# A transformer layer on one core: where the rotary products of the queries stand, and which engine takes the last query tile

## The reference

```python
q = (hidden_states @ wq).reshape(B, S, H, D)
k = (hidden_states @ wk).reshape(B, S, Hkv, D)
v = (hidden_states @ wv).reshape(B, S, Hkv, D)
q = q * cos + _rotate_half(q) * sin
k = k * cos + _rotate_half(k) * sin
scores = jnp.einsum('bqkgd,bskd->bkgqs', qg, k) * scale
attn = jax.nn.softmax(scores, axis=-1)
out = jnp.einsum('bkgqs,bskd->bqkgd', attn, v).reshape(B, S, E)
x = _layernorm(x + out @ wo)
x = _layernorm(x + _L0_ffn_ref(x, ...))
```

## Time and profile before

| what | us |
|---|---|
| median of 3 runs | 897.87 |
| lowest and highest run | 894.81, 898.11 |
| the profiled execution, its own time | 896.11 |
| span of the profiled execution | 894.3 |
| busy in the span: TensorE (matmul) | 876.0 |
| VectorE | 743.9 |
| ScalarE | 711.1 |
| GpSimd | 268.9 |

### The profile page before, as it was taken

The page is one execution under the profiler, slowest core; times in us unless marked ns, Lnnn a source line. Parts: engine busy times, 40 slices in busy tenths (PEclk is TensorE's granted clock), DMA queues, the critical chain, the costliest instruction groups (busy, mean ns, idle before and its releaser), DMA issues.

```text
span 894.3 us, 16211 instructions
## 1 busy us (share of the span) xinstructions
PE 876.0 (98%) x5658; PEld 457.9 (51%) x5658; DVE 743.9 (83%) x1655; ACT 711.1 (80%) x929; POOL 268.9 (30%) x232
## 2 busy tenths in 40 slices
PE   9999999999999999999999999999999999999996
PEld 3334444444444444434444444444436888888885
DVE  5688999999999999999999999999955455665545
ACT  2466999999999999999999999999985466555564
POOL 6564430045334010001001000210104665665555
PEclk9997999999999999999999999999999999999998
DMA  8874543423342122122223212121112010110001
GB/s 301 251 208 103 148 116 89 98 73 86 103 115 58 46 77 71 52 70 67 53 60 82 74 43 78 45 69 31 35 55 57 25 49 24 48 48 25 25 24 48
DMA packets 53458, 69.98 MB, mean 78 GB/s; under 512 B 17344, under 2 KB 26560, under 8 KB 53376
## 3 DMA queue, kind: packets, MB, share of 16 engines
q1 hardware_dynamic: 50280, 65.53, 26.4%
q0 software_dynamic: 864, 3.15, 1.1%
q10 hardware_dynamic: 2232, 0.25, 0.2%
HBM read 46.74 MB, written 16.25 MB: 70 GB/s over the span
## 4 chain that ended last, share of the span: by engine, by line
PE 89%; DVE 5%; ACT 2%; SPq 2%; DMA 2%; issue 1%; POOL 0%; POOLq 0%; DVEq 0%
PE pv_bank L1395 27%; PE ring_bank L1305 24%; PE pair_bank L1454 13%; PE pair_bank L1524 12%; PE pv_bank L1550 3%; PE ring_bank L1550 3%; PE ring_bank L1405 2%; DVE block_max L869 2%; PE pair_bank L1343 1%; ACT probs L1203 1%; DMA ident<-identity 1%; PE ring_bank L1420 1%; DMA k_max<-k_parts 0%; PE pair_bank L1305 0%; DVE inv_sums L962 0%
## 5 line engine op out<-in xcount | busy, mean ns | idle before, releaser
L1203 ACT ACTIVATE probs<-pair_bank 128x1024 f32<-128x1024 f32 x512 | 495.9, 1024 | 45.6 <-PE pair_bank L1454 45.5
L869 DVE TENSOR_REDUCE block_max<-ring_bank 128x1 f32<-128x384 f32 x854 | 486.5, 609 | 14.4 <-PE ring_bank L1305 4.1
L1305 PE MATMUL ring_bank<-k_max,q_sb 48*128 48x512 f32 x1122 | 310.1, 443 | 3.8 <-DVE block_max L865 2.6
L1305 PEld LDWEIGHTS ring_bank<-k_max,q_sb 48*128 48x128 f32 x1122 | 149.1, 185 | 267.1 <-DVE block_max L869 119.7
L1395 PE MATMUL pv_bank<-probs,v_all 128*17 128x512 f32 x2048 | 271.4, 602 | 0.7 <-ACT probs L1203 0.7
L1454 PE MATMUL pair_bank<-q_sb,k_sb 50*128 50x512 f32 x1024 | 221.5, 427 | 0.8 <-ACT probs L1203 0.7
L1063 DVE SCALAR_TENSOR_TENSOR hid<-pair_bank,up_s,silu 128x512 f32<-128x512 f32 x63 | 47.1, 748 | 85.1 <-ACT silu L1265 85.1
L1454 PEld LDWEIGHTS pair_bank<-q_sb,k_sb 50*128 50x128 f32 x1024 | 98.5, 186 | 27.2 <-ACT probs L1203 6.4
L774 POOL TENSOR_TENSOR hid_l<-hid,hid_h 128x512 fp32r<-128x512 f32 x63 | 81.7, 1296 | 86.4 <-ACT hid_h L1244 85.7
L689 POOL TENSOR_TENSOR attn<-attn,inv_rows 128x1024 f32<-128x1024 f32 x7 | 16.7, 2388 | 300.8 <-DMA inv_rows<-inv_d 300.8
L865 DVE CUSTOM_DVE_ANT_0 above<-ring_bank,above 128x512 f32<-128x512 f32 x128 | 88.1, 689 | 5.0 <-ACT above L1151 4.9
(11 more groups left out here) (147 smaller groups left out, 862.9 us busy)
## 6 DMA issues: line engine op xcount, KB each, us to landing
k_max<-k_parts SPq DMA_DIRECT2D x96, 96.0 KB, 3.1
q_sb<-q_parts SPq DMA_DIRECT2D x64, 128.0 KB, 2.8
k_sb<-k_parts SPq DMA_DIRECT2D x96, 64.0 KB, 2.4
attn<-xT SPq DMA_DIRECT2D x8, 512.0 KB, 7.6
q_parts<-high SPq DMA_DIRECT2D x16, 256.0 KB, 3.6
q_parts<-low SPq DMA_DIRECT2D x16, 256.0 KB, 3.9
q_sb<-q_parts SPq DMA_DIRECT2D x64, 64.0 KB, 2.9
attn<-pv_sb SPq DMA_DIRECT2D x128, 32.0 KB
```

Source lines behind the costliest of these rows:

```text
L869: dve.reduce_max(block_max[half % 2][:, col:col + 1], bank[:, 0:width], axis=AX.X).then_inc(ring_used, 1)
L1203: act.activation(probs[t % 2][:, 2 * pr:2 * pr + 2, :], pair_bank[pr][:], ACT.Exp, scale=D ** -0.5).then_inc(probs_ready, 1)
L1305: pe.matmul(bank[:, 0:last - first], q_sb[k][rows, i, qt * P:(qt + 1) * P], k_max[k // QH][rows, kind * CH + first:kind * CH + last], star ...
```

## The change

It has four pieces.

1. In every step of the prologue VectorE does the products of a query half ahead of the maxima of the same place, not after them. ScalarE copies V and K rows of tiles 3, 5 and 7 before high_part of the tile before (it was after it).
2. The second half of the last query tile isn't multiplied by VectorE. ScalarE copies pv_bank to q_last in SBUF (copy_q_last, after hook 3 of tile 7). GpSimd makes the two products (products_last), rotates, rounds (high_last) and subtracts. The first P x V waits for the copy.
3. The four early banks are taken in another order, so that the last two differences that ScalarE takes lie in pair_bank[1]; the second scores of step 0 wait for these two. In step 0 TensorE issues them ahead of max block 1.
4. On GpSimd products_k(1) moves behind turn 1. On SyncE the wait for all query stores and swap_strips(1) move behind load_shift(0, 1); the stores of tile 7 go out high parts first.

```diff
         q_bank = [pair_bank[0][:, 0, :], pair_bank[0][:, 1, :]]
-        early_banks = [ring_bank[0][:], ring_bank[1][:], pair_bank[1][:, 1, :], pair_bank[1][:, 0, :]]
+        early_banks = [ring_bank[1][:], pair_bank[1][:, 1, :], pair_bank[1][:, 0, :], ring_bank[0][:]]
         k_bank, v_bank = ring_bank[2], pv_bank
...
         def bank_index(pos):
-            return pos % EARLY_BANKS if pos < early_entries else (0, 1, EARLY_BANKS)[pos % BANKS]
+            return pos % EARLY_BANKS if pos < early_entries else (3, 0, EARLY_BANKS)[pos % BANKS]
...
                 cols = slice(c * CH, (c + 1) * CH)
-                for part, buf, ready, count in [((0, high, hi_ready, 2 * m + j + 1), (1, low, lo_ready[j], m + 1))[q] for q in parts]:
+                highs = (0, high, last_high_ready, j + 1) if m == BLOCKS - 1 else (0, high, hi_ready, 2 * m + j + 1)
+                for part, buf, ready, count in [(highs, (1, low, lo_ready[j], m + 1))[q] for q in parts]:
                     sp.wait_ge(ready, count)
...
                             load_kv(0, 1)
-                            swap_strips(1)
-                        store_q(m, 0)
-                        store_q(m, 1)
+                            for part in range(2):
+                                store_q(m, 0, (part,))
+                                store_q(m, 1, (part,))
+                        else:
+                            store_q(m, 0)
+                            store_q(m, 1)
                     if m == 2:
...
-            for slot in range(4):
-                sp.wait_ge(stored[slot], 16 * 2 * B)
-            sp.wait_ge(v_used, 2 * B)
+            def prologue_over():
+                for slot in range(4):
+                    sp.wait_ge(stored[slot], 16 * 2 * B)
+                sp.wait_ge(v_used, 2 * B)
...
                         load_shift(p + 1, 0)
+                    if first and k == 0:
+                        prologue_over()
+                        swap_strips(1)
                     if first and k < B - 1:
...
+            def products_last():
+
+                cols = slice(CH, S)
+                pool.wait_ge(q_last_ready, 1)
+                pool.wait_ge(q_tables_loaded[1], 16 * 2)
+                pool.wait_ge(rot_ready, 2 * (BLOCKS - 1))
+                pool.tensor_tensor(by_sin[0][:], q_last, sinq_sb[:, cols], ALU.mult).then_inc(q_last_parts, 1)
+                pool.tensor_tensor(by_cos[1][:], q_last, cos_sb[:, cols], ALU.mult).then_inc(q_last_parts, 1)
+
             def rotate(m, j):
-                pool.wait_ge(parts_ready, Q_PARTS * m + 3 + j)
+                if m == BLOCKS - 1:
+                    pool.wait_ge(parts_ready, Q_PARTS * m + 2)
+                    pool.wait_ge(q_last_parts, j + 1)
+                else:
+                    pool.wait_ge(parts_ready, Q_PARTS * m + 3 + j)
                 if m:
...
                     after_turn(0)
-                pool.wait_ge(hi_ready, 2 * m + j + 1)
+                if m == BLOCKS - 1:
+                    pool.wait_ge(last_high_ready, j + 1)
+                else:
+                    pool.wait_ge(hi_ready, 2 * m + j + 1)
                 pool.tensor_tensor(low[slot][:], rotated[j][:], high[slot][:].bitcast(fp32), ALU.subtract).then_inc(lo_ready[j], 1)
...
+            def high_last(j):
+                slot = 2 + j
+                pool.wait_ge(rot_ready, 2 * (BLOCKS - 1) + j + 1)
+                pool.wait_ge(stored[slot], 16 * 2 * (B - 1))
+                pool.tensor_copy(high[slot][:], rotated[j][:]).then_inc(last_high_ready, 1)
+
             for m in range(BLOCKS):
+                if m == BLOCKS - 1:
+                    products_last()
                 rotate(m, 0)
                 rotate(m, 1)
+                if m == BLOCKS - 1:
+                    high_last(0)
+                    high_last(1)
                 if m == 0 or m % 2 or m >= FIRST:
...
                     rotate_k(0)
-                if m == BLOCKS - 2:
-                    products_k(1)
+            after_turn(1)
+            products_k(1)
             for b in range(1, B):
...
                     low_first(m - 1)
+                rotary_q(m, 0)
                 early_maxima(m, 2)
-                rotary_q(m, 0)
                 early_maxima(m, 3)
-                early_maxima(m, 4)
                 if m < BLOCKS - 1:
                     rotary_q(m, 1)
+                early_maxima(m, 4)
                 early_maxima(m, 5)
...
                         turn_shift(before)
-                    if n == 3 and g == 0:
-                        rotary_q(BLOCKS - 1, 1)
                     if key:
...
+            def copy_q_last():
+                act.wait_ge(proj_ready, 3 * BLOCKS)
+                act.activation(q_last, pv_bank[:], ACT.Copy).then_inc(q_last_ready, 1)
+
             def take_v(b):
...
                     gap_high()
+                if c and b:
+                    copy_v_rows(b)
+                    copy_k_rows(b)
                 if m:
...
                 early_takes(m, 1)
-                if c:
-                    if b:
-                        copy_k_rows(b)
-                    copy_v_rows(b)
+                if m == 1:
+                    copy_v_rows(0)
                 early_takes(m, 2)
...
                     early_takes(m, h)
+                    if (m, h) == (BLOCKS - 1, 3):
+                        copy_q_last()
...
                                 difference(*maxima_at(g))
-                            if (g, pr) == (2, 1):
-                                high_part(BLOCKS - 1, 0)
-                            if (g, pr) == (3, 1):
-                                high_part(BLOCKS - 1, 1)
                             if n + 1 < HALVES * PAIRS:
...
                 if g == 0:
-                    pe.wait_ge(parts_ready, Q_PARTS * BLOCKS)
+                    pe.wait_ge(q_last_ready, 1)
                 if t == 0 and not first_use:
...
                                 if pr:
-                                    for index in range(2, EARLY_BANKS):
+                                    for index in (1, 2):
                                         pe.wait_ge(*taken(last_in(index, early_entries)))
...
                             maxima(0)
-                            maxima(1)
                             scores(1)
-                            for i in range(2, len(entries)):
+                            for i in range(1, len(entries)):
                                 maxima(i)
...
                             maxima(0)
```

More of the change, by code:

```diff
@@ L108, in layer @@
         by_sin = [sb(f"by_sin{c}", [P, CH], fp32, one) for c in range(2)]
+        rotated = [sb(f"rotated{c}", [P, CH], fp32, one) for c in range(2)]
+        q_last = attn[:, FIRST, 0:CH]
+        key_signs = sb("key_signs", [P, HKV * D], fp32, one)
+        high = [sb("high0", [P, CH], f32r, one)]
         v_rows = [sb(f"v_rows{c}", [P, CH], fp32, one) for c in range(2)]
-        rotated = [sb(f"rotated{c}", [P, CH], fp32, one) for c in range(2)]
-        key_signs = sb("key_signs", [P, HKV * D], fp32, one)
-        high = [sb(f"high{c}", [P, CH], f32r, one) for c in range(4)]
+        high += [sb(f"high{c}", [P, CH], f32r, one) for c in range(1, 4)]
         low = [sb(f"low{c}", [P, CH], f32r, one) for c in range(4)]
@@ L194, in layer @@
         k_gap_ready = sem("k_gap_ready")
+        q_last_ready, q_last_parts, last_high_ready = sem("q_last_ready"), sem("q_last_parts"), sem("last_high_ready")
         k_stored = [sem(f"k_stored{b}") for b in range(B)]
```

## The result

| | before | changed |
|---|---|---|
| median of 20 runs each, us | 896.56 | 899.28 |
| lowest and highest | 894.57, 899.18 | 895.75, 902.0 |
| profiled execution: own time, span | 896.11, 894.3 | 895.75, 893.9 |
| mean granted clock of the profiled execution | 0.991 | 0.995 |

The ratio of the changed kernel to the kernel before is 1.0031 (95% interval 1.0023 to 1.0040): **slower by 0.3%, some 2.8 us**. The prediction was 897.7 for a kernel at 897.87, no change, with 0.2 us won. The measured change is a loss, and its interval does not reach 1.

The account below looks back on a forecast made before the run. The prediction took the kernel to be bound by TensorE's stream; 6.1 us won up to turn 1 less 4.6 for SyncE's queue gave 1.5, taken as 0.2 for the clock: about 897.7, no measurable change (0.55), range 895 to 900.

Parts of the forecast that it names:

- Part 1: Prologue, query products ahead of maxima and earlier V and K copies: counted zero, bounds 0.7 lost and 0.5 won.
- Part 2: Banks and last query tile at steps 0 and 1: step 1's scores at 68.0, 1.75 us earlier.
- Part 4: SyncE's queue after turn 1: a new 2.8 us stall at step 16; the way to step 24 is 4.6 longer.
- T: The end of turn 1 on VectorE, from which the queue is counted; forecast 79.0, before 85.12.
- Part 3: Clock at steps 0 and 1: no fall, at 4 in 5, winning 4.4 us besides the 1.75.
- the lost half-clock stretch: Steps 1 to 5 took 13.83 us where the later pace gives 9.44; the episode cost 4.4.
- The term: Lead up to turn 1: 4.4 from the clock together with 1.75 from step 1, 6.1 us earlier.
- The sum: 6.1 won less 4.6 for the queue: 1.5 us won if the clock holds in the stalls, 0.2 taken.
- my middle: Clock after the stall at step 16, bounds 0 and 4.4: between 1.5 won and 1.1 lost, 0.2 won taken.
- Rival B: Clock still falls before step 5, only 1.75 won, queue takes 4.6: 2.9 lost, median 900.8; chance 0.20.
- Rival A: SyncE's queue is in time, no stall at steps 16 and 24: all 6.1 remain, median 891.8; chance 0.18.
- Rival C: Clock holds at step 16 and falls at step 24: 2.9 lost, 900.8; chance 0.07.

Follow-up runs that it names:

- The fourth experiment: The changed kernel with products_k(1), swap_strips(1) and the order of the prologue put back as before; 893.51 us, ratio 0.9964 to the kernel before.
- The first experiment: The changed kernel with products_k(1) and swap_strips(1) put back where they were; 893.51 us, ratio 0.9965 to the kernel before.
- The ninth experiment: The first experiment plus one extra matmul of 256 columns ahead of the second scores in step 0; 892.65 us, ratio 0.9966 to the kernel before.
- the fifth experiment: The changed kernel plus two unread matmuls ahead of the wait for the shift in steps 16 and 24; 897.49 us, ratio 1.0013 to the kernel before.
- The second experiment: The kernel before with only products_k(1) moved behind turn 1 and swap_strips(1) behind the shift of half 1; 902.64 us, ratio 1.0069.
- the seventh experiment: The changed kernel with SyncE's shifts of halves 2 and 3 ahead of swap_strips(2) and swap_strips(3); 900.75 us, ratio 1.0042 to the kernel before.
- sixth: The first experiment plus extra matmuls in step 0, 256 columns ahead of the second scores and 128 behind each later max block; 892.37 us, ratio 0.9953.

## Why the prediction was wrong

**Part 1 (prologue: zero) held.** The fourth experiment puts it at nothing that can be told. The first scores came at 64.15, forecast 64.4, and the loss in tile 5 that the bounds allowed for is there: TensorE was held up near 46, and part of it was won back.

**Part 2 (banks, last tile) held.** Second scores at 65.41 (forecast 65.4), step 1 at 68.17 (68.0). GpSimd was done at 72.9 (bound 74), and nobody waited for it.

**Part 4 (the queue) held to 0.6 us**, as the numbers behind T show, and the first two experiments confirm that it is the cause of the loss: with the keys early the stalls are gone, with the keys late alone they come to the kernel before. What I gave as 4.6 from turn 1 to step 24 measured 128.56 - 80.43 - 43.46 = 4.67.

**Part 3, the clock at the hand-over, is the step that failed.** I wrote: "So I expect no fall, at 4 in 5", because TensorE would idle about 1.0 us of the 3.6 from 64.4 on. The idle time came nearly as forecast (2.47 us busy in 64.4 to 68.0, so 1.1 idle), and the clock fell all the same, to 0.55 in 69 to 72. So it was not the chain to step 1 that was wrong but what I concluded from it. With the fall, the 4.4 that I put on the lost half-clock stretch was not to be had in full. In the best trace the stretch was shorter, and step 5 came 83.58 - 79.14 = 4.4 earlier, of which 1.6 were already there at step 1 and 2.9 are clock. Over many executions it is less. The first experiment shows the lead alone, with no stall behind it: 3.1. The term stood at 6.1, twice as much. The ninth experiment shows that the size was fair for a clock that holds, 5.6 at step 5 in its trace, and that the clock is what was missing: its executions with the higher mean clock are 2.8 faster than the others. The two rows that I had for it (42% idle with a fall, 45% without one) contradict each other already, and I still took 28% as safe. They were slices of 3 us besides, and the 1.16 us for which TensorE idled before 66.32 in the kernel before lay mostly in the slice ahead of the one I read. What decides between a fall and none stays open.

**The sum.** The measured lead and the queue make 3.1 - 4.7 = 1.6 lost; the fifth experiment, which has the queue's delay and little of the clock behind it, has 1.2 lost (0.0013 of 896). The clock behind the stalls adds 1.6, between the bounds of 0 and 4.4; my middle amounted to 1.3. The last two add up to the measured 2.8 because they are differences of the same ratios; with the 1.6 from the lead and the queue it is 3.2, so 0.4 is left over. A second way agrees: the queue's 4.6 and the clock's 1.6 make 6.2, and that is what the two moves cost the kernel before (6.2) and nearly what they cost the changed one (5.9). So the queue and the clock behind it were sized rightly, and the error of 3.0 (0.2 won, 2.8 lost) is the lead, 3.1 in place of 6.1.

The time itself, 899.28, lies inside my range of 895 to 900. That is luck: the range stood around a kernel at 897.87, which 20 runs put at 896.56, and the loss is real. I had also said that a measurement can tell only 4.5 us from no change; with 20 runs of each the interval is 2.1 to 3.6 us.

Rival B named the mechanism: the clock still falls before step 5, the queue takes its 4.6. Its 2.9 lost is almost the measured 2.8, but partly by luck: it had 1.75 for the lead (3.1 measured) and nothing for the clock behind the stalls (1.6), and the two errors nearly cancel. A middle case, a fall that ends sooner, was in neither the forecast nor the rival. Rival A (the queue in time) is ruled out by the trace. Rival C (a fall at step 24 and none at step 16) can't be told apart from falls at step 16, since the changed kernel's trace has neither.

The Trainium skill, TensorE: Matmul & The Clock Gate, section HAM oscillation — how this bites in real kernels, tells of waits for a DMA after which TensorE ran at the lower clock. The second experiment's trace agrees (0.62 busy in 111 to 114, clock 0.54 in 114 to 117); the changed kernel's own trace has two such waits and the clock stays at 1.00 (1.10 busy in 105 to 108, 0.84 in 126 to 129). Both happen with the same kind of stall.

## What to carry to other kernels

Before a transfer is moved behind another one in a queue, lay the queue out from the event that starts it to the next deadline of the busiest engine. Here that sum, from issue and landing times, was right to 0.6 us, and it says that swap_strips(1) should stay in the time that SyncE had to spare: the change without that move and that of products_k(1) beats both kernels (0.9965). Count a wait for a round trip (DMA, addition, DMA) inside the queue as a piece of its own: it held SyncE for 2.87 us in the changed kernel and 3.85 in the seventh experiment, where the issue of four DMAs takes 2.3 to 2.7. And don't book a clock stretch as won because a hole gets smaller: keep both ends, since it was worth half its price here, and look at the mean clock of many executions, not at one trace.

## What the runs showed of the hardware

The clock fell at the hand-over with TensorE recorded as busy 2.40 of 3.00 us (changed kernel) and 2.32 (first experiment); it stayed up with 2.97 (sixth), and once with 2.38 (ninth). It did not fall behind the stalls in the changed kernel's trace (1.10 and 0.84 of 3.00 busy), and it did behind one in the second experiment's (0.62). The mean clocks of the other executions, 0.986 to 0.993, speak for such falls in many of them, and the times spread with it: 895.75 to 902.0 for the changed kernel, 895.75 to 898.28 with the stalls filled. Two matmuls of pure waste, recorded as 1.98 us inside a wait, made a kernel faster at the median. Casting a turn's rows on VectorE took 0.71 us at 54.61 in the changed kernel, while GpSimd was subtracting (54.01 to 55.29), and 0.17 at 77.94, where GpSimd was idle:

```profile
54.61 0.71 DVE L915 CAST shift_rows<-row_max 128x16 fp32r<-128x16 f32 x1
...
77.94 0.17 DVE L915 CAST shift_rows<-row_max 128x16 fp32r<-128x16 f32 x1
```

The Trainium skill, SBUF — State Buffer, section Who interferes with whom, says that a VectorE cast can be held up whole while GpSimd has the ports that they share. The trace agrees: the cast ends at 55.32, with the subtraction. It happened in the prologue and in both kernels (0.74 at 54.11 in the kernel before), so it has no part in the difference between them.
